# An attention and mixture-of-experts block on one core: routing behind the maxima, bias sums in the first expert slots, a finish in halves, and the last four heads divided on chip

## What is computed

```python
scores = einsum(q, k) * scale + lam * (einsum(q_cos, k_cos) + einsum(q_sin, k_sin)) * scale
attn = softmax(where(causal, scores, -inf))
x = layernorm(x + einsum(attn, v).reshape(b, s, d) @ Wo)

gating = softmax(x @ Wg + bg)                 # 8 experts, the two best are taken
h = silu((x @ W1[e] + b1[e]) * (x @ W3[e] + b3[e]))
mixed = sum over the two experts of gate * (h @ W2[e] + b2[e])
out = layernorm(x + mixed @ Wf + bf)
```

## Time and profile before

| | |
|---|---|
| median of 3 runs | 1869.32 us (1865.62 to 1869.4) |
| the profiled execution's own time | 1874.46 us |
| its span | 1872.8 us |
| TensorE busy | 1705.1 us, 91% |
| VectorE busy | 1261.6 us, 67% |
| ScalarE busy | 887.2 us, 47% |
| GpSimd busy | 344.0 us, 18% |
| mean granted TensorE clock | 0.959 of full |

### The profile page before, as it was taken

The page is one execution under the profiler, slowest core; times in us unless marked ns, Lnnn a source line. Parts: engine busy times, 40 slices in busy tenths (PEclk is TensorE's granted clock), DMA queues, the critical chain, the costliest instruction groups (busy, mean ns, idle before and its releaser), DMA issues.

```text
span 1872.8 us, 28046 instructions
## 1 busy us (share of the span) xinstructions
PE 1705.1 (91%) x8954; PEld 870.7 (46%) x8955; DVE 1261.6 (67%) x3115; ACT 887.2 (47%) x1036; POOL 344.0 (18%) x477
## 2 busy tenths in 40 slices
PE   6999989999999999999999999988179999999955
PEld 3544444444444444444444434433146666666544
DVE  3699887787787777786877867852335555555536
ACT  2876765555555556565565455545112222222126
POOL 0000021121211212212221131141211111111231
PEclk9999989999999999999999999989689999999978
DMA  3465444030110222220220200631741111111134
GB/s 108 158 233 183 158 143 148 6 105 11 39 71 7 69 75 77 75 81 30 98 80 21 95 30 7 192 91 63 267 133 46 45 45 45 45 45 45 43 129 157
DMA packets 104971, 163.70 MB, mean 87 GB/s; under 512 B 11136, under 2 KB 65184, under 8 KB 104480
## 3 DMA queue, kind: packets, MB, share of 16 engines
q1 hardware_dynamic: 89312, 126.76, 20.7%
q0 software_dynamic: 15552, 35.56, 5.6%
HBM read 92.10 MB, written 69.54 MB: 86 GB/s over the span
## 4 chain that ended last, share of the span: by engine, by line
PE 69%; DVE 6%; ACT 5%; DMA 5%; issue 3%; SPq 1%; POOL 1%; ACTq 0%; DVEq 0%; POOLq 0%
PE att_ps_s L1152 22%; PE exp_ps_h L1843 13%; PE att_ps_o L1171 12%; PE att_ps_m L274 9%; PE exp_ps_y L1861 6%; ACT att_probs L1208 3%; DMA att_sums<-att_out_t 2%; DVE att_maxima L284 2%; PE att_ps_m L1542 2%; PE exp_ps_t L1851 2%; DMA route_a_inv<-inv_rows 1%; PE exp_ps_x L1832 1%; DVE fin_stats L1340 1%; DVE fin_res L2078 0%; PE fin_ps_y L1385 0%
## 5 line engine op out<-in xcount | busy, mean ns | idle before, releaser
L1208 ACT ACTIVATE att_probs<-att_ps_s 128x1024 f32<-128x1024 f32 (+3 forms) x640 | 561.6, 895 | 472.3 <-PE att_ps_s L1152 459.4
L1152 PE MATMUL att_ps_s<-att_queries,att_keys 49*128 49x512 f32 (+3 forms) x2560 | 622.5, 558 | 32.6 <-ACT att_probs L1208 22.0
L284 DVE TENSOR_REDUCE att_maxima<-att_ps_m 128x1 f32<-128x512 f32 x768 | 487.3, 684 | 114.4 <-PE att_ps_m L274 111.0
L274 PE MATMUL att_ps_m<-att_keys,att_queries 48*128 48x512 f32 (+3 forms) x1280 | 482.3, 578 | 17.5 <-DVE att_maxima L284 7.7
L274 PEld LDWEIGHTS att_ps_m<-att_keys,att_queries 48*128 48x128 f32 x1280 | 189.2, 186 | 311.0 <-DVE att_maxima L284 150.5
L1152 PEld LDWEIGHTS att_ps_s<-att_queries,att_keys 49*128 49x128 f32 x2560 | 238.5, 190 | 154.2 <-ACT att_probs L1208 102.8
L287 DVE CUSTOM_DVE_ANT_0 att_ps_m<-att_ps_m,att_future 128x128 f32<-128x128 f32 (+3 forms) x512 | 241.2, 513 | 71.7 <-PE att_ps_m L274 70.0
L1171 PE MATMUL att_ps_o<-att_probs,att_values 128*32 128x512 f32 (+3 forms) x2560 | 274.5, 544 | 0.5 <-POOL att_probs L1284 0.4
L1843 PE MATMUL exp_ps_h<-keep_w,exp_rows_t 128*128 x568 | 258.3, 598 | 5.7 <-DVE exp_rows_t L1877 5.7
L1919 ACT ACTIVATE exp_hidden<-exp_product 128x512 f32<-128x512 f32 x71 | 44.8, 632 | 344.4 <-DVE exp_product L1902 344.4
L1284 POOL TENSOR_SCALAR_AFFINE_SELECT att_probs<-att_probs 128x512 f32<-128x512 f32 x128 | 83.1, 649 | 409.8 <-ACT att_probs L1208 409.5
(11 more groups left out here) (187 smaller groups left out, 1377.6 us busy)
## 6 DMA issues: line engine op xcount, KB each, us to landing
att_queries<-q_parts SPq DMA_DIRECT2D x64, 192.0 KB
att_keys<-k_parts SPq DMA_DIRECT2D x64, 192.0 KB
exp_rows<-sorted_rows SPq DMA_DIRECT2D x71, 129.0 KB, 2.3
v_rows<-pre_v_sb SPq DMA_DIRECT2D x8, 1024.0 KB, 4.7
q_parts<-pre_waves SPq DMA_DIRECT2D x16, 512.0 KB, 5.3
k_parts<-pre_waves SPq DMA_DIRECT2D x16, 512.0 KB, 6.2
att_values<-v_rows SPq DMA_DIRECT2D x32, 256.0 KB
out_parts<-att_out_t POOLq DMA_DIRECT2D x32, 256.0 KB, 5.9
```

Source lines behind the costliest of these rows:

```text
L274: pe.matmul(bank[:, 0:width], self.queries[g % 2][half, c, r, P * q:P * q + P], self.keys[g % 2][half, k, r, 0:width], start=True, stop=Tr ...
L284: dve.tensor_reduce(to, bank[:, 0:width], AX.X, ALU.max).then_inc(self.s_mr, 1)
L1152: mm = pe.matmul(score_tile(unit, first, last)[:, e], keys[g % 2][half, k // TPC, r, P * (k % TPC):P * (k % TPC) + P].bitcast(F32), querie ...
L1208: act.activation(probs[:, step % PROBS, DUO * r:DUO * r + DUO, first:last], score_tile(unit, first, last), ACT.Exp, scale=SCALE).then_inc( ...
```

## The change

Four parts.

1. The planner lets no route from number 4 on begin while maxima are still to be sent (`route_due`).
2. The last quad's four heads of the last chunk do not go through memory. Their sums are spread over the partitions by one matmul with a 0/1 matrix (`sum_row`, an event `own_sums` for TensorE), VectorE takes the reciprocal of 128x512 and multiplies, and SyncE moves four blocks of 16 partitions by 2 KB within the on-chip memory into the operand of the projection. The other twelve heads are loaded and divided ahead (`load` for number 7 waits for attention chunk 27). The store of sums, result and inverse for chunk 31 is gone. The semaphores of the two products made once are merged into one pair.
3. `add_bias` stands in slots 2 to 5 in place of 66 to 69.
4. In the finish the picks and the stores are split in two halves of two 128-row tiles, the weight load stands behind the first chunk's picks, and TensorE's two steps of an iteration change places.

```diff
-RING_KINDS = ("max", "turn_max", "fold_turn", "fold", "project", "count")
+RING_KINDS = ("max", "turn_max", "fold_turn", "fold", "own_sums", "project", "count")
+LAST_ROUTE = ROUTE[:1] + [("own_sums",)] + ROUTE[1:]
...
     def keep_inverse(self):
...
-        if g % NQ == NQ - 1:
+        if n == CHUNKS - 1 - QC:
+            self.arrived[NCH - 1] = self.free["pe"] + LOADED
+        elif g % NQ == NQ - 1:
...
     def route_due(self):
-        if self.routed not in self.arrived:
+        if self.routed not in self.arrived or self.routed >= QC and self.group < len(self.groups):
             return None
...
     def route_ready(self):
         due = self.route_due()
-        if due is None or self.route_steps()[self.at_step][0] not in RING_KINDS:
+        if due is None or self.route_steps()[self.at_step][0] == "own_sums" and self.value < QUADS * STEPS:
+            return None
+        if self.route_steps()[self.at_step][0] not in RING_KINDS:
             return due
...
             for i in range(QC + 1, NCH - 1):
                 routing.load(sp, i, s_store, s_kept)
                 routing.keep_rows(sp, i - 1)
+            routing.load(sp, NCH - 1, s_store, s_kept)
             routing.keep_rows(sp, NCH - 2)
-            routing.load(sp, NCH - 1, s_store, s_kept)
+            routing.move_own(sp, out_t[:, (CHUNKS - 1) % 2], range(QUAD))
             sp.wait_ge(s_pv, QUADS * STEPS)
...
+                elif event == "own_sums":
+                    pe.wait_ge(s_oc, CHUNKS)
+                    routing.spread_sums(pe, take(), out_t[:, (CHUNKS - 1) % 2])
...
             def store(g, s):
-                if ends_chunk(s):
+                if ends_chunk(s) and g * STEPS + s < QUADS * STEPS - 1:
...
     def load(self, sp, i, s_store, s_kept):
-        last = ((i // QC + 1) * NQ - 1) * QC + i % QC
+        quads_in = NQ if i < NCH - 1 else NQ - 1
+        last = (i // QC * NQ + quads_in - 1) * QC + i % QC
...
+    def spread_sums(self, pe, bank, own):
+        pe.wait_ge(self.s_zeros, 5)
+        pe.matmul(bank[:, :], self.sum_row[:, :], own, start=True, stop=True).then_inc(self.s_once, 1)
+
+    def divide_own(self, dve, bank, own):
+        inverse = self.wo_t[:, :].rearrange("p k d -> p (k d)")
+        dve.wait_ge(self.s_once, self.SPREAD)
+        dve.reciprocal(inverse, bank[:, :]).then_inc(self.s_seen, 1)
+        dve.wait_ge(self.s_seen, self.SPREAD)
+        dve.tensor_tensor(own, own, inverse, ALU.mult).then_inc(self.s_own, 1)
+
+    def move_own(self, eng, own, heads):
+        eng.wait_ge(self.s_own, 1)
+        for h in heads:
+            first = P // 2 + HD * h
+            eng.dma_start(self.a_raw[first:first + HD, DK - 1], own[VW * h:VW * h + HD]).then_inc(self.s_moved, 16)
...
     def project(self, pe, bank, i, t):
         if t == 0:
-            pe.wait_ge(self.s_at, i + 1)
+            pe.wait_ge(self.s_at, i + 1 + (i == NCH - 1))
+        if i == NCH - 1:
+            pe.wait_ge(self.s_moved, 16 * QUAD)
...
+        if i == NCH - 1:
+            for k, rows in enumerate((P, P // 2)):
+                dve.tensor_tensor(self.a_raw[0:rows, k], self.a_raw[0:rows, k], self.a_inv[0:rows, k], ALU.mult).then_inc(self.s_at, 1)
+            return
         dve.tensor_tensor(self.a_raw[:, :], self.a_raw[:, :], self.a_inv[:, :], ALU.mult).then_inc(self.s_at, 1)
...
             def add_bias(s, p):
-                first = SLOT_TILES - 1 - NCH // 2
+                first = 2
...
             for p in range(4):
                 sp.wait_ge(mixed_rows.s_out[p], 16 * len(range(p, SLOT_TILES, 4)))
-            sp.dma_start(wf[:, :], Wf.rearrange("(k p) n -> p k n", p=P)).then_inc(s_w, 16)
             def load(i, p):
...
-                for r in range(TOPK):
-                    sp.dma_start(picked[:, p, r], at(rows_in[r], i)).then_inc(s_pick[p], 16)
-            pipelined(sp, NCH, [(load, 0)])
+                for h in range(2):
+                    part = slice(h * TPC // 2, (h + 1) * TPC // 2)
+                    for r in range(TOPK):
+                        sp.dma_start(picked[:, p, r, part], at(rows_in[r], i)[:, part]).then_inc(s_pick[p][h], 16)
+                if i == 0:
+                    sp.dma_start(wf[:, :], Wf.rearrange("(k p) n -> p k n", p=P)).then_inc(s_w, 16)
+            pipelined(sp, NCH, [(load, 0)], unrolled=True)
...
             def store(i, p):
-                pool.wait_ge(norm.s_done, i * TPC + TPC)
-                pool.dma_start(at(rows_out, i), normed[:, p]).then_inc(s_out[p], 16)
+                for h in range(2):
+                    part = slice(h * TPC // 2, (h + 1) * TPC // 2)
+                    pool.wait_ge(norm.s_done, i * TPC + (h + 1) * TPC // 2)
+                    pool.dma_start(at(rows_out, i)[:, part], normed[:, p, part]).then_inc(s_out[p], 16)
...
-            pipelined(pe, NCH, [(turn, 0), (project, 1)])
+            pipelined(pe, NCH, [(project, 1), (turn, 0)])
```

74 lines of the change are left out of this document (44 added, 30 removed).

## The result

The changed kernel takes **1855.57 us** (median of 6, 1852.48 to 1860.74); the one before, beside it on the same chip, 1867.59 (6 runs, 1863.48 to 1871.68). The ratio is 0.9931, 95% [0.9909, 0.9952]: 9 to 17 us faster. The forecast was 1857.2. The time was met; of its four terms only the one of the bias sums came near.

The account below looks back on a forecast made before the run. TensorE was taken to bound attention and experts, except at four places the change touches. Terms -5.3 - 7.1 - 2.2 + 2.5 = -12.1 took 1874.46 to 1862.4; against the median of 1869.32, 1857.2 us, range 1848 to 1868.

Parts of the forecast that it names:

- maxima first: End of the attention: chunk 31's maxima row is ready early, removing its wait and some low clock; -5.3 us, bounds -12 to +4.
- last heads on chip: Behind the attention: on-chip path replaces 16.4 us from copy to projection by 9.3; -7.1 us, bounds -9.6 to -4.3.
- passed on: Behind the attention: the whole 7.1 us gained before the projection also reaches the later pads and weights.
- sums early: Experts: moving bias sums gains 10.2 us in the tail and loses 8.0 in early slots; net -2.2 us.
- finish: Finish: TensorE's new order slows the chunks, partly offset by shorter start and end; net +2.5 us, bounds -2.5 to +6.
- ring: Finish: transposition, copy and projection of a chunk follow each other strictly, 5.7 us a chunk over VectorE's 5.21.
- the last window: End of the attention: 58.5 us at mean clock 0.91, about 5 us lost to low clock, 1.7 of it recovered.
- three spells: End of the attention: low-clock stretches in the 121 us, costing about 3.3, 0.8 and 5 us.
- ScalarE's stops: End of the attention: routes 4 and 5 interrupt ScalarE without maxima as filler, losing 0.9 us each, 1.8 together.
- Route 6's eight: GpSimd, attention's end: these puts move behind the masks but stay hidden, as route 7's places come about 23 us later.
- Rival C: Behind the attention: DMA queues hold pads and weights, only 2 us of the short cut pass through; 1862.3 us, chance 0.10.
- Rival B: Finish: it keeps 5.2 us a chunk because VectorE is full; 1852.2 us in all, chance 0.10.

Follow-up runs that it names:

- experiment 3: Changed kernel without the clause that makes routes wait for the maxima, the rest kept: 1867.68 us, ratio 0.9998 to the kernel before.
- experiment 1: Kernel before with one edit, routes from number 4 on wait until the last maxima group is issued: 1862.62 us, ratio 0.9966.
- experiment 2: Kernel before with the maxima first, plus route 6's puts on GpSimd issued behind the store of the last inverse rows: 1858.1 us, ratio 0.9955.
- experiment 9: Changed kernel with the 4 MB of W2 issued behind the pads and the first two row blocks: 1864.0 us, ratio 0.9982 to the kernel before.
- experiment 12: Changed kernel with single bias sums on VectorE, transposition first in the finish, W2 behind four row blocks and ahead of kept rows: 1833.06 us, ratio 0.9832.
- Experiment 7: Changed kernel with one bias sum in each of eight slots instead of two in four, still on GpSimd: 1852.04 us, ratio 0.9924 to the kernel before.
- experiment 5: Changed kernel, but in the finish TensorE transposes the next chunk before projecting the current one: 1850.78 us, ratio 0.9914 to the kernel before.

## Why the prediction was right, and where it was not

| term | forecast | traces | what the step had wrong |
|---|---|---|---|
| maxima first | -5.3 | -17.7 (after), -16.1 (alone), -10.9 (after against all but the maxima) | low clock and idle time, both too small |
| last heads on chip | -7.1 | -6.9 + 2.8 = -4.1 | "passed on" in full |
| sums early | -2.2 | +7.8 - 8.7 = -0.9 | the tail, 1.5 too large |
| finish | +2.5 | +6.7 | ring without ScalarE's root |
| sum | -12.1 | -16.0 (with -17.7) | times: -12.0 |

Against the kernel before, three of the four are outside the bounds that the forecast gave them: -17.7 against -12, -4.1 against -4.3, +6.7 against +6.

**The maxima.** The mechanism stood: the wait of 3.2 us for the row is gone, and idle time fell by 8.6. The size failed in two places. One is the sentence "which I put at a third of the 5 us that the last window lost so, 1.7". The busy time of equal work fell by 9.2 against before and by 4.6 against experiment 3, 122.6 to 118.0: the low clock went from more than a third of one window. The other is the idle time, -6.2 + 1.8 + 0.8 = -3.6 in the forecast and -8.6 or, against experiment 3, -6.3 in the traces. Of the 12.4 us by which the term missed -17.7, the clock is 7.5 and the idle time 5.0. My own reading of the earlier trace rows had the material, three spells with 9 us of lost work in 121; I left two of them standing, and they only made the bound of -12. The cost of 1.8 for ScalarE's stops didn't appear (6.9 us of waits against 7.3). And one queue was not followed far enough: "Route 6's eight now lie behind the masks" is true, but the last two stores stand on GpSimd too, and there the puts cost 4 to 5 us: experiment 1 has 4.9 more than before, experiment 2 takes 4.2 of them back. The changed kernel doesn't pay it, because the last heads no longer use these stores. So two edits that I had added up separately meet on one queue. In the times they look as if they needed each other: all without the maxima is level with before (0.9998), all without the own heads is level too (0.9993), and both together are 13 us faster. Beyond the puts this isn't shown. By the five later stages, against the mean of the two traces of before, the maxima alone are worth 10.2 us, all without them 5.6, and both together 15.9, about their sum.

**The last heads.** The step was nearly exact: 9.5 us for 9.3. The reciprocal took 3.37 for the forecast's 3.2 from the slope of two narrow rows, or 6.6 ns a column over 512. The estimate of 4.3, worked out from the repeat count of 8 in the Trainium skill (VectorE: DVE Perf Modes), is too high here. Rival C was right in part: it let 2 us through, and 4.1 of the 6.9 came through, while 2.8 were lost again at the queue that it named. Experiments 9 and 12 show that the pads wait behind the 4 MB of W2: without these 6.4 and 6.8 us go. That the same queue made the difference of 2.8 between before and after is argued from the traces, not shown by a run of its own. I had compared when the weights' issue starts in the two kernels, but not how far ahead of the pads it ends: from 1309.5 (its start is at 1299.48, six issues) to the first pad's at 1316.06 are 6.5 us now, 8.6 before. From the first weights' issue to the first pad's it is 16.6 us now and was 23.4 (1323.25 to 1346.68), with the same 8 MB in between.

**The sums.** As forecast the loss moved and didn't go: four slots, 1.95 us each. Experiment 7 shows the other side: a sum that ends where the product begins costs nothing (0.69 us for the product), while the bias additions that read PSUM run beside it in their usual 0.69. Both agree with the rule that the forecast cites from the Trainium skill (SBUF — State Buffer, Who interferes with whom), an exclusive lock between a VectorE instruction with two SBUF inputs and a GpSimd instruction that reads SBUF. What I didn't ask was whether the pair was needed. One sum a slot gives 7.9 us of the stage.

**The finish.** The ring of 5.7 us is there in four of seven steps (5.69 to 5.77). In the step of 6.69 ScalarE's copy stood behind its norm, the norm behind the root and a table load, and the root behind the copy of the chunk before. TensorE waited 2.10, its clock fell, the projection took 5.40 instead of 3.72, and so the next step took 7.45. The first step took 7.43 behind a projection that also ran at a low clock. The forecast listed transposition, copy and projection, and left out what stands ahead of the copy in ScalarE's own order; the table load and the low clock at the start it had only in its bound of +6. Rival B, 5.2 us a chunk, is wrong for this order; with the old one (experiment 5) it would have been right.

The errors, -12.4 or -10.8 (-5.6 against experiment 3) in one term against +3.0, +1.3 and +4.2 in the others, largely cancelled, and the stages of the traced executions are 3 to 4 us further apart than the times. That the forecast hit within 2 us is luck; what was right is the direction, and the wait and the blocked product that two of the terms rest on.

**Left open.** For each of the twelve changed kernels the sum of the five later stages is 3 to 8 us further below before than the times are (5.5 in the mean: the changed one -15.9 by its trace against the mean of the two of before, -12.9 by its ratio; the last one -36.7 and -31.3). Both traced executions of before were slower than its usual ones (1874.46 and 1872.6, medians 1866.2 to 1869.5), though their first 1170 us were average. It may be that most executions of before do the stretch in some 139 us and the traced ones happened not to. Experiment 3 shows that the order of before can do it in 137.2, and this would explain the 5.5; that most executions of the kernel before itself do so isn't shown.

## What to carry to other kernels

Give the low clock a term of its own: compare the busy time for an equal number of matmuls, not only the idle time, and when a change removes the waits of a stretch, ask whether all of its low-clock time goes and not only the spell behind the wait. When a reordering moves work on a queue, follow it to the end of the stage, to the last store that anybody waits for, and price edits that share a queue together and not one by one. Take two traces of the kernel before, and one of a variant with the same order, before calling a low-clock time a cost of the order. Where two instructions can't run beside each other, like the product and GpSimd's sum here, look for the piece that fits the gap before moving the pair elsewhere.

## What the runs showed of the hardware that I had not expected

An issue on SyncE isn't of constant cost: the same four loads of 1 MB took 16.62 us to issue in experiment 9 and 6.00 in experiment 12. The DMA engines' share was 0.97 and 0.90 in these stretches. In the first GpSimd issued its eight loads of the kept rows just ahead (from 1334.45), in the second it had to wait until W2 had landed; whether that is the reason isn't shown. A reciprocal of 128x512 with its input in PSUM runs at 6.6 ns a column and takes nearly five times as long as the product of the same size (3.37 and 0.70). The same TensorE order had its low-clock spells at different places in three traces and cost 144.0, 143.9 and 137.2 us. A 128x1024 addition takes 1.22 us on VectorE and 2.37 on GpSimd.
